# Loading order of lora_A and W, first Ax, table of combined W chunks and the seventeenth sample's rearrangement in a conv + LoRA FFN kernel

## The reference

```python
# x: (32, 128, 2048); conv: 4 groups, 9 taps, padding 4
y = conv(x, weight) + (c @ c_weight.T)[:, :, None] + bias[None, :, None]
# rows of y have length 2048: y @ kernel, plus a LoRA of rank 32 per batch of four samples and a shared one
A_eff = einsum('bn,nri->bri', gate, lora_A)       # 16 LoRAs mixed by gate
B_eff = einsum('bn,nor->bor', gate, lora_B)
out = x + y @ kernel + ffn_bias + (y @ A_eff.T) @ B_eff.T + (y @ lora_A_shared.T) @ lora_B_shared.T
```

## Time and profile before

| | us |
|---|---|
| median of 3 runs (lowest, highest) | 1742.2 (1741.74, 1744.91) |
| the profiled execution's own time | 1747.0 |
| its span, first to last instruction | 1745.2 |
| PE busy in it | 1722.7 (99%) |
| DVE, ACT, POOL busy | 987.1, 669.9, 36.1 |
| mean granted TensorE clock | 0.996 of full |

### The profile page before, as it was taken

One profiled execution on the slowest core, in us unless ns is written; L12 is line 12 of the kernel. 1 busy time (PEld: TensorE's weight loads), 2 busy tenths in 40 slices (PEclk: granted clock), 3 DMA queues, 4 the chain that ended last, 5 costly groups with the idle time before them and its releaser, 6 DMA issues.

```text
span 1745.2 us, 21990 instructions
## 1 busy us (share of the span) xinstructions
PE 1722.7 (99%) x8666; PEld 1460.6 (84%) x8666; DVE 987.1 (57%) x1260; ACT 669.9 (38%) x846; POOL 36.1 (2%) x70
## 2 busy tenths in 40 slices
PE   9999999999999999999999999999999999999998
PEld 6778888887888889999999888888888888888887
DVE  7647766664444578777665544355455554464443
ACT  6656666654222376555561221132233211121110
POOL 0001200000000000000000000000000000000000
PEclk9999999999999999999999999999999999999999
DMA  7859876656665656766665676568667798887764
GB/s 229 249 152 334 291 260 234 230 201 196 225 226 198 226 204 258 271 254 241 247 244 200 213 247 222 188 200 269 217 224 228 274 333 303 305 322 259 241 240 158
DMA packets 180143, 419.48 MB, mean 240 GB/s; under 512 B 50692, under 2 KB 90212, under 8 KB 175400
## 3 DMA queue, kind: packets, MB, share of 16 engines
q1 hardware_dynamic: 169960, 381.22, 64.1%
q0 software_dynamic: 9216, 33.56, 5.2%
q10 hardware_dynamic: 864, 3.29, 0.5%
HBM read 271.97 MB, written 146.03 MB: 240 GB/s over the span
## 4 chain that ended last, share of the span: by engine, by line
PE 89%; DMA 5%; DVE 3%; ACT 1%; issue 1%; SPq 0%; POOL 0%; ACTq 0%; DVEq 0%
PE acc L1430 65%; PE cps L1306 15%; PE acc L1337 3%; PE cps L1353 3%; DMA g<-in_L_ffn_kernel 2%; DMA T<-g 1%; DMA g<-in_L_ffn_lora_A 1%; ACT x_q L688 1%; PE acc L1385 1%; PE cps L1370 1%; DMA mixed_A<-g 1%; DVE x_q L946 0%; DMA st<-in_L_ffn_kernel 0%; DMA b_raw<-shared_B 0%; PE cps L1363 0%
## 5 line engine op out<-in xcount | busy, mean ns | idle before, releaser
L1430 PE MATMUL acc<-w_hi,y_t 128*128 128x512 f32 x3584 | 996.0, 392 | 1.8 <-DVE w_lo L938 1.8
L1430 PEld LDWEIGHTS acc<-w_hi,y_t 128*128 128x128 f32 x3584 | 666.5, 188 | 138.4 <-issue 2.7
L1430 PE MATMUL acc<-w_lo,y_t 128*128 128x512 f32 x1792 | 553.8, 390 | 0.0
L1430 PEld LDWEIGHTS acc<-w_lo,y_t 128*128 128x128 f32 x1792 | 337.2, 188 | 71.5
L688 ACT COPY x_q<-x_raw 32x512 f32<-32x512 f32 x248 | 268.4, 1082 | 16.2 <-DVE x_lo L952 13.4
L1306 PE MATMUL cps<-cw_hi,x_hi 128*128 128x384 f32 (+2 forms) x768 | 229.7, 299 | 3.3 <-DVE ax L1085 2.6
L1063 DVE TENSOR_TENSOR g<-acc,g 128x1024 f32<-128x1024 f32 x96 | 117.2, 1222 | 203.8 <-PE acc L1337 116.7
L1306 PE MATMUL cps<-cw_lo,x_hi 128*128 128x384 f32 (+2 forms) x768 | 229.8, 299 | 0.0
L1306 PE MATMUL cps<-cw_hi,x_lo 128*128 128x384 f32 (+2 forms) x768 | 229.2, 298 | 0.0
L727 ACT CAST y_t<-g 128x1024 fp32r<-128x1024 f32 x95 | 100.1, 1054 | 334.8 <-PE acc L1430 305.4
L1023 DVE TENSOR_TENSOR y_t<-g,y_t 128x1024 fp32r<-128x1024 f32 x95 | 116.0, 1221 | 109.8 <-ACT y_t L727 109.6
(11 more groups left out here) (117 smaller groups left out, 940.7 us busy)
## 6 DMA issues: line engine op xcount, KB each, us to landing
g<-A SPq DMA_DIRECT2D x80, 512.0 KB, 4.7
g<-U SPq DMA_DIRECT2D x80, 512.0 KB, 6.2
A<-g SPq DMA_DIRECT2D x64, 512.0 KB, 4.8
g<-in_x SPq DMA_DIRECT2D x64, 512.0 KB, 6.3
out<-g SPq DMA_DIRECT2D x64, 512.0 KB, 3.5
x_raw<-in_x SPq DMA_DIRECT2D x31, 1024.0 KB, 5.2
U<-g SPq DMA_DIRECT2D x48, 512.0 KB, 3.9
g<-in_L_ffn_kernel POOLq DMA_DIRECT2D x32, 512.0 KB, 8.6
```

The costliest lines, as they stand in the source:

```text
L1430: ins = T.matmul(acc[:, b, m, :], y_buf[b][:, c, part, :], wt[:, k % SLOTS, m * 512:(m + 1) * 512], start=(c == 0 and part == 0 and wt is ...
```

## The change

Five edits:

1. SP issues W chunks 6 and 7 ahead of lora_A part 0. lora_A has four buffers now: parts 0 and 1 in g as before, parts 2 and 3 in the W ring `st`, so part 2 waits for W chunk 5's split (w_lo_ready 6) and part 3 for chunk 7's (w_lo_ready 8), where both waited for the first four mixes. Part 2 is issued ahead of x(2), part 3 behind it. The mixes 4 to 7 are copied into g[2] and g[3], not `st`, and no longer wait for w_lo_ready.
2. POOL's first quarter loads wait for all eight transposes and for both stores of the first half of mixed A, not for the mixes and x(3).
3. In step 1, ACT rearranges x(3) ahead of the evacuation of product(0), and both ACT and DVE do a_split(0) ahead of x_split(3).
4. FORM_AT: form(3, 1) goes from step 5 to step 6, ahead of form(4, 0). All other halves stay.
5. `next_x`: the seventeenth sample (v = 16) is loaded in step 28 and rearranged in step 29, not 29 and 30. Its split stays in step 30.

```diff
@@ tables
-FORM_AT = {u: ((u - 2, 0), (u - 2, 1)) for u in range(2, 6)} | {u: ((u // 2 + 1, u % 2),) for u in range(6, 14)}
+FORM_AT = {2: ((0, 0), (0, 1)), 3: ((1, 0), (1, 1)), 4: ((2, 0), (2, 1)), 5: ((3, 0),), 6: ((3, 1), (4, 0))} | {
+    u: ((u // 2 + 1, u % 2),) for u in range(9, 14)} | {7: ((4, 1),), 8: ((5, 0),)}
@@ buffers
-        la_raw = [g[:, 2 + 2 * b:4 + 2 * b, :].rearrange("p a n -> p (a n)") for b in range(2)]
+        la_raw = [buf.rearrange("p a n -> p (a n)") for buf in (g[:, 2:4, :], g[:, 4:6, :], st[:, 0:2, :], st[:, 2:4, :])]
-        mixed = [buf[:, i * 512:(i + 1) * 512] for buf in (b_raw, b_raw, st[:, 0], st[:, 1]) for i in range(2)]
+        mixed = [buf[:, i * 512:(i + 1) * 512] for buf in (b_raw, g[:, 2], g[:, 3]) for i in range(2)]
+        mixed = mixed[0:2] + mixed
@@
+        def next_x(u):
+            if u in (2 * NP - 3, 2 * NP - 2):
+                return NP if u == 2 * NP - 3 else None
+            return conv_index(u + 2) if has_conv(u + 2) else None
@@ SP
-                    sp.wait_ge(amix_done, 4)
-                sp.dma_start(la_raw[k % 2], lora_A[:, k * R8:(k + 1) * R8, :]).then_inc(la_in[k], 16)
+                    sp.wait_ge(w_lo_ready, 2 + 2 * k)
+                sp.dma_start(la_raw[k], lora_A[:, k * R8:(k + 1) * R8, :]).then_inc(la_in[k], 16)
@@ SP, before step 1
             load_t(0, 5)
-            load_lora_A(0)
             load_t(0, 6)
             load_t(0, 7)
+            load_lora_A(0)
             load_lora_A(1)
             store_y(0)
+            load_lora_A(2)
             load_x(2)
+            load_lora_A(3)
             sp.wait_ge(ctx_out, 16)
             load_ctx(2)
             store_mixed_A(0, 0)
-            load_lora_A(2)
-            load_lora_A(3)
             store_mixed_A(0, 1)
@@ SP, step u
-                if has_conv(u + 3):
-                    load_x(conv_index(u + 3))
+                if next_x(u + 1) is not None:
+                    load_x(next_x(u + 1))
@@ POOL
-                    pool.wait_ge(amix_done, 2 * 4)
-                    pool.wait_ge(x_in, 16 * 4)
+                    pool.wait_ge(aturn_done, 2 * 4)
+                    pool.wait_ge(amix_out[0], 16 * 2)
@@ ACT, copy_mixed_A
-                elif n == 4:
-                    act.wait_ge(w_lo_ready, NCH)
@@ ACT, step u
+                if u == 1:
+                    x_rearrange(3)
                 if pf == 0:
                     act.wait_ge(main_done, u)
...
-                if has_conv(u + 2):
-                    x_rearrange(conv_index(u + 2))
-                    x_split(conv_index(u + 2))
                 if u == 1:
                     a_split(0)
+                if u > 1 and next_x(u) is not None:
+                    x_rearrange(next_x(u))
+                if has_conv(u + 2):
+                    x_split(conv_index(u + 2))
@@ DVE, step u
-                if has_conv(u + 2):
-                    x_rearrange(conv_index(u + 2))
+                if next_x(u) is not None:
+                    x_rearrange(next_x(u))
                 if has_conv(u + 1):
                     y_evacuate(conv_index(u + 1))
+                if u == 1:
+                    a_split(0)
                 if has_conv(u + 1) and (u + 1) // NP == 2:
                     sums(u + 1)
                 if has_conv(u + 2):
                     x_split(conv_index(u + 2))
-                if u == 1:
-                    a_split(0)
@@ PE, mix_A
-                                   la_raw[k].rearrange("p (w t) -> p w t", t=WIN)[:, :, 4 * j:4 * j + 4],
+                                   la_raw[2 * i + k].rearrange("p (w t) -> p w t", t=WIN)[:, :, 4 * j:4 * j + 4],
```

## The result

| | before | changed kernel |
|---|---|---|
| median of 8 runs each, on the same chip, us | 1741.55 | 1747.37 |
| lowest and highest, us | 1740.12, 1744.91 | 1745.75, 1749.16 |
| ratio, 95% interval | | 1.0032 [1.0021, 1.0043] |
| the profiled execution's own time, us | 1747.0 | 1745.75 |

The change makes the kernel 5.8 us slower. 1739.7 was predicted, so the sign was wrong, though 1747.4 lies inside the range. The last line of the table holds the first clue: the two profiled executions say -1.3 us, the medians +5.8. The profile of before lies above every one of the eight runs of before in this comparison, that of the changed kernel is the lowest of its eight. Two single executions further on, one of r9 (5372.5 us) and one of the kernel before beside it (3437.5 us), are left out of every range and ratio; the medians count them.

A forecast was written before the change was run, and what follows sets the result against it. PE, busy 1722.7 of 1745.2 us, was taken as the bound, so only its idle time and low clock could move. The terms -8.7 - 4.3 + 10.5 = -2.5 gave 1744.5, or 1739.7 us on the median; range 1733 to 1748.

The forecast's parts named there:

- start, edits 1 to 3: Start of the kernel up to the first Ax: waits and low clock go, -0.8 - 1.0 - 4.2 - 2.7 = -8.7 us.
- steps 5 and 6, one half fewer in step 5: PE's waits in steps 6 and 7 (0.7, 0.8, 0.2 us) go once form(3, 1) leaves step 5: -1.8 us.
- step 7: stall, b_raw, low clock: PE waits for y_evacuate(8) behind chunk 4's reload: 8.8 us stall, 0.8 for b_raw, 2.7 of low clock.
- edit 4, the last two: Combined chunks, form(3, 1) moved to step 6: +8.8 + 0.8 + 2.7 - 1.8 = +10.5 us.
- edit 5: Seventeenth sample: the 2.65 us wait before conv(16) and 1.65 us of low clock go, -4.3 us.
- W ahead of lora_A: First mixes: W chunk 6's 1.8 us wait goes, lora_A part 1 lands at 40 to 42; gain 0.8, ends 1.8 and -1.
- If PE waits over 2 us for L1394's lora_A part 1: Sign at the mixes of the start: such a wait would show the prediction wrong in its start.
- lora_A part 3: Later mixes: issued near 44, it lands near 57, ahead of its mix, so a 1.0 us wait goes.
- The first Ax: Step 1: ACT rearranges earlier, so PE's 4.2 us wait goes, with 2 us of room, and 2.7 of low clock.
- the rival built on that pace: Chunk 4's reload at an empty queue's pace, 6.8 us by the skill's rule, 6.7 taken: -5.8, 1736.4 us; chance 0.20.
- The slow reload: Chunk 4's reload in step 6 takes 14.5 us or more: +3.8, 1746.0 us; chance 0.18.
- the start gains half: Start: lora_A part 1 or x(2) comes late and a low clock appears elsewhere: +2, 1744 us; chance 0.09.

The follow-up runs named there:

- r9: Kernel before with only POOL's first quarter loads made to wait for the transposes and first-half mixed A stores; 1742.47 us, ratio 0.9994.
- r5: Kernel before, unchanged, profiled once more; that execution took 1741.46 us.
- r2: Changed kernel with the old FORM_AT table, so form(3, 1) back in step 5; 1737.41 us, ratio 0.9966.
- r4: Kernel before with only the seventeenth sample loaded and rearranged a step sooner; 1738.6 us, ratio 0.9982.
- r3: Kernel before with only the new FORM_AT table, form(3, 1) in step 6; 1752.41 us, ratio 1.0055.
- r8: r2 with step 1 of ACT and DVE back in its old order; 1738.62 us, ratio 0.9969.
- r6: r2 with lora_A part 0 again loaded ahead of W chunks 6 and 7; 1735.51 us, ratio 0.9957.
- r7: r6 with a FORM_AT table that spreads the halves, each chunk's first half a step behind the previous chunk's last; 1730.98 us, ratio 0.9932.
- r11: r7 with the lora_A change undone wholly (two buffers, old load order, parts 2 and 3 late); 1733.4 us, ratio 0.9946.
- r1: Kernel before, unchanged, profiled again; 1745.65 us.
- r10: r4 with the spread FORM_AT table of r7; 1734.12 us, ratio 0.9954.

## Why the prediction was wrong

The failed step is the sentence on the start, "So 4.2 us go, with 2 us of room, and the low clock with it", together with the sentence that the sum "is made against it, and its difference is then put on the median". I had noted that the profiled execution took 4.8 us more than the median and did not ask where those 4.8 lay. They lay in this very wait and in the clock behind it. Of the 6.9 us booked, r5 shows 0.2 us of wait and full clock. Such executions are not rare: 10 of the 69 of the kernel before in the four comparisons took 1747.0 us or more, and three of the six profiles without edit 2 have 1.9 us or more of this wait. But the result is taken on the median, and that lies among the others.

| term | predicted | profiled pair | on medians |
|---|---|---|---|
| start, edits 1 to 3 | -8.7 | -6.2 | -1.2 (r2 less r4, some 4 us of doubt each way) |
| steps 5 and 6, one half fewer in step 5 | -1.8 | -2.6 | |
| step 7: stall, b_raw, low clock | +12.3 | +11.8 | |
| edit 4, the last two | +10.5 | +9.2 | +10.1 (r3) |
| edit 5 | -4.3 | -4.3 | -3.7 (r4) |
| sum | -2.5 | -1.3 | +5.2; measured +5.8 |

- **W ahead of lora_A.** "I take 0.8 us of gain" was mis-sized. W's wait went as predicted (the first mix started at 39.03, not 41.27), and part 1 was used at 42.48, close to the 40 to 42 of the forecast. But PE had to stand still for it, 2.4 to 3.2 us in one piece (changed, r2, r8), and each time the clock fell behind that; for this wait the sum had no term of clock. The mixes' pair at 42.48 took 2.07 us instead of 1.02, and conv(1) started at 52.37, not 50.27: 2.1 us of loss against the profile of before, where 0.8 of gain was booked. By the medians of r2 and r6 it is a loss of 1.9, with the doubt named above. My bound on that side was 1 us of loss. "If PE waits over 2 us for L1394's lora_A part 1" was named as the sign of an error in the start, and it came.
- **lora_A part 3.** The 1.0 us wait is gone, as said.
- **The first Ax.** The mechanism was right: L696 ahead of L886, no wait, clock 1.00 from 91 to 97. I had a_parts on DVE near 84 and PE at 86.2, and PE came at 88.09; product(0) was that much later, by the lora_A wait above (mix_B of step 0 at 73.15, where I counted on 70.6 to 71.4). Only what it replaces was wrong.
- **Edit 4.** Right in mechanism, and in the size of the whole. DVE's idle time before L1020 is 13.96 us (about 13 said), from the end of form(3, 1) at 219.94 to POOL's first load at 224.85 are 4.9 us (4.8 taken), from there to the last landing 9.04 (8.2), PE waited 9.64 (8.8), and the clock was 0.50 from 241 to 245. Step 7 took 35.65 us against 23.34 undisturbed (r7), so 2.7 us are clock (2.7 taken). The 0.8 for b_raw behind the stall did not come: the one wait of that size stands in step 5, at 187.68. That the stall was 0.8 longer made up for it, which is luck. The Trainium skill (DMA: Bandwidth & Descriptors, section Anatomy of one DMA) gives 6.8 us for those loads as an estimate, with the four counted as one DMA; the measured 9.04 decides against it here, and against the rival built on that pace.
- **Edit 5.** Right. No wait in front of conv(16), clock 1.00 at 623 us.
- **The rivals.** The slow reload had the right sign for another reason. The right case, a start whose gain exists only in some executions, was not among them: "the start gains half" was as near as I came, and its condition, a late lora_A part 1 with a low clock behind it, did occur.

With 0.8 or 1.2 for the start in place of 8.7, the same sum gives +5.0 to +5.4.

## What to carry to other kernels

Two kinds of wait look alike in one profile. The one here that is set by the order of an engine's work came out the same in five executions (2.64 to 2.65 us); the one at whose root a DMA's landing stands came out anywhere from 0.17 to 4.21 us. Before a wait of the second kind is booked it should be set against the gap between the profiled execution and the median, or seen in a second execution. Where a buffer's reload needs its stores to have landed, what matters is on which step the asking engine asks. With a step between the two, a round trip of 19.8 us cost DVE 1.28 us and PE nothing (r7); side by side, one of 13.96 us cost PE 9.64 and 2.7 of clock.

## What the hardware showed that I had not expected

- The same store, issued 68.3 to 72.3 us into the execution with POOL's loads 1.6 to 2.1 us behind it, landed after 4.9 to 9.4 us in six executions of code that is alike up to there.
- The clock after an idle stretch of PE did not follow from the length of that stretch alone. At W chunk 6, idle times of 2.8 (r11), 2.9 (r7), 3.05 (r6) and 3.5 us (r1) were followed by a granted clock of 0.50 to 0.63 in the 2 to 4 us behind them, but 2.8 (r10) and 3.1 us (r4) by 1.00 throughout. Here the stretches behind that wait in r4:

```profile
38.00:40.00 2.00, 1.65 (x6) 1.05 (x6) 1.45 (x5) 1.97 (x2) 0.00 (x0) 1.00 1.03 233
40.00:42.00 2.00, 1.63 (x7) 1.37 (x8) 1.96 (x4) 0.18 (x1) 0.00 (x0) 1.00 0.90 303
```

And the same two stretches of r6:

```profile
38.00:40.00 2.00, 1.82 (x6) 1.01 (x5) 1.71 (x2) 1.38 (x2) 0.00 (x0) 0.63 0.99 217
40.00:42.00 2.00, 2.00 (x6) 1.54 (x6) 1.93 (x5) 0.00 (x0) 0.00 (x0) 0.52 0.98 389
```

- Shorter idle times than these were also followed by a fall: 2.43 us (changed kernel, 0.53 from 43 to 46 us) and, in step 5 of r6, 1.99 us, where r5's 1.55 us at W chunk 6 and r1's 1.92 us before the first Ax were followed by 1.00. In front of conv(16) 2.64 us of idle time lowered the clock in every profile in which it occurred (before, r1, r3, r5, r9). PE of r6 in step 5, and the clock behind it:

```profile
184.78 1.61 PE L1361 MATMUL cps<-y_t,a_parts 128*128 128x256 f32 x8 [1.99 <-DVE g L970]
```

```profile
186.00:188.00 2.00, 2.00 (x7) 1.61 (x7) 2.00 (x3) 1.47 (x3) 0.00 (x0) 0.50 1.05 428
```

- One more draw stands ahead of all edits. At the start of product(0) the clock was 0.50 from 26 to 28 us in the profile of before, where r10's was 1.00; it was low near there in before, the changed kernel, r2, r3, r5 and r9, and full in the other seven. Among the kernels with W last, those with the low clock waited 1.3 to 1.6 us for W chunk 6 and those with the full one 2.8 to 3.5: PE came sooner, and the chunk did not. So the length of that wait says little on the order of the loads.
